# Four graph layers on one core: an attention chunk's accumulators gated while they are copied, drains replaced by semaphores, degrees in three batches

## The reference, cut to what matters

```python
deg = jnp.clip(adj.sum(axis=1), 1.0)
dis = deg ** (-0.5)
adj_norm = dis[:, None] * adj * dis[None, :]
diffusion = adj_norm @ x - x
sim = x @ x.T / (norms[:, None] * norms[None, :])
attn = jax.nn.softmax(beta * sim * adj, axis=1)
return diffusion + jax.nn.sigmoid(alpha) * (attn @ x - x)
```

## Time and profile before

| What | Value |
|---|---|
| median of three runs | 945.01 us (944.57 to 945.73) |
| the profiled execution | 945.11 us, its span 943.3 us |
| mean granted TensorE clock over the span | 0.992 of full speed |
| PE busy | 856.4 us, 91% of the span |
| DVE busy | 642.5 us, 68% |
| ACT busy | 485.7 us, 51% |
| POOL busy | 292.1 us, 31% |
| read from HBM | 69.81 MB |

### The profile page before, as it was taken

One profiled execution on the slowest core, in us unless ns is written; L12 is line 12 of the kernel. 1 busy time (PEld: TensorE's weight loads), 2 busy tenths in 40 slices (PEclk: granted clock), 3 DMA queues, 4 the chain that ended last, 5 costly groups with the idle time before them and its releaser, 6 DMA issues.

```text
span 943.3 us, 18224 instructions
## 1 busy us (share of the span) xinstructions
PE 856.4 (91%) x6496; PEld 509.7 (54%) x6496; DVE 642.5 (68%) x1782; ACT 485.7 (51%) x1020; POOL 292.1 (31%) x380
## 2 busy tenths in 40 slices
PE   0189999999999999979999999999999999999992
PEld 0157676767676767645444445555455555545451
DVE  6989999999999999994344423322135676646576
ACT  5758687878687877653122212111026646525344
POOL 4665454544344544432111210000012222212121
PEclk9999999999999999999999999999999999999996
DMA  8848887988798989200000000000000000000100
GB/s 248 241 125 261 203 247 222 237 226 263 199 251 208 246 224 236 62 1 1 1 1 1 1 1 1 1 1 1 1 1 1 1 1 1 1 1 13 34 23 23
DMA packets 84813, 89.75 MB, mean 95 GB/s; under 512 B 71296, under 2 KB 76544, under 8 KB 76544
## 3 DMA queue, kind: packets, MB, share of 16 engines
q1 hardware_dynamic: 81088, 88.09, 33.7%
q10 hardware_dynamic: 3648, 0.61, 0.4%
HBM read 69.81 MB, written 2.10 MB: 76 GB/s over the span
## 4 chain that ended last, share of the span: by engine, by line
PE 53%; DVE 25%; issue 10%; POOL 4%; DVEq 3%; ACT 2%; DMA 1%; ACTq 0%; POOLq 0%; SPq 0%
PE ps_acc L1234 27%; PE ps_acc L1166 10%; DVE e_parts L762 6%; PE ps_s L1149 6%; DVE ps_s L756 4%; PE ps_t L1234 3%; PE ps_t L1149 3%; POOL att_sb L356 2%; DVE ps_t L756 2%; PE ps_s L1297 1%; DVE ez L689 1%; POOL e_parts L332 1%; PE ps_s L1265 1%; ACT ez L480 1%; DVE x L779 1%
## 5 line engine op out<-in xcount | busy, mean ns | idle before, releaser
L332 POOL CAST e_parts<-ez 128x512 f16<-128x512 f32 x256 | 158.0, 644 | 201.7 <-ACT ez L480 201.7
L1166 PE MATMUL ps_acc<-h_a,e_parts 128*128 128x129 f16 x3072 | 198.6, 220 | 21.6 <-DVE e_parts L762 20.8
L1166 PEld LDWEIGHTS ps_acc<-h_a,e_parts 128*128 128x128 f16 x3072 | 183.7, 97 | 61.4 <-DVE e_parts L762 33.1
L1234 PE MATMUL ps_acc<-adj_t,stage 128*128 128x512 fp8e4 x896 | 198.9, 379 | 0.0
L762 DVE TENSOR_TENSOR e_parts<-ez,e_parts 128x512 f16<-128x512 f32 x256 | 178.3, 735 | 10.3 <-POOL e_parts L332 9.5
L1234 PE MATMUL ps_acc<-adj_t,h_a 128*128 128x512 fp8e4 x768 | 170.3, 379 | 0.0
L434 ACT ACTIVATE bytes<-stage 128x1024 uint8<-128x1024 f32 x128 | 134.1, 1048 | 28.1 <-DMA stage<-in_adj 28.0
L1234 PEld LDWEIGHTS ps_acc<-adj_t,stage 128*128 128x128 f16 x896 | 87.1, 98 | 98.9
L1149 PE MATMUL ps_s<-u_t 128*128 128x512 f16 x516 | 127.0, 383 | 0.0
L480 ACT ACTIVATE ez<-ps_s,scal 128x1024 f32<-128x1024 f32 x86 | 103.1, 1199 | 42.4 <-DVE ps_s L756 40.7
L518 ACT ACTIVATE ez<-x,small 128x128 f32 (+1 forms) x96 | 39.5, 482 | 158.9 <-DVE small L881 158.9
(11 more groups left out here) (164 smaller groups left out, 830.8 us busy)
## 6 DMA issues: line engine op xcount, KB each, us to landing
stage<-in_adj SPq DMA_DIRECT2D x64, 1024.0 KB, 5.7
x<-in_x SPq DMA_DIRECT2D x4, 512.0 KB, 8.3
out<-x SPq DMA_DIRECT2D x8, 256.0 KB, 2.2
adj_t<-bytes SPq DMA_TRANSPOSE x64, 3.1
kernel_sb<-in_L_gnn_kernel ACTq DMA_DIRECT2D x1, 64.0 KB, 7.1
w_sb<-in_L_gnn_W ACTq DMA_DIRECT2D x1, 64.0 KB, 8.1
embed_top<-in_L_gnn_embed ACTq DMA_DIRECT2D x1, 64.0 KB, 8.2
embed_top<-in_L_gnn_layer ACTq DMA_DIRECT2D x1, 64.0 KB, 7.4
```

The costliest lines, as they stand in the source:

```text
L332: g.tensor_copy(e_parts[:, HI, g_s % RING, :], ez[:, g_s % RING, :]).then_inc(ehi_done, 1)
L1166: last = t.matmul(att_acc[:, b, 0:D + 1], e_parts[:, re, g_s % RING, P * b:P * (b + 1)], h_a[:, s, rh, 0:D + 1], start=(s == 0 and n == 0 ...
L1234: last = t.matmul(acc, h[:, k, r, :], adj_f8[:, k // 2, CW * c:CW * (c + 1), k % 2], start=(k == 0 and r == LO), stop=(k == NB - 1 and r = ...
```

## The change

Seven things are done. (1) The evacuation takes the reciprocal of the denominators from the accumulators, and copies the accumulators with the gate `sig_h` applied; both release `acc_free`, so PE's waits count by two. (2) It stands behind the first of the pair's two low parts instead of ahead of both. (3) The tail has only the four updates of `x`; waits on `acc_free`, `x_less` and the new `x_att` take the place of its drains. (4) `x_minus_h` signals `x_less` and has no drain; ACT waits for all eight of them before it casts the quarter that leads to the overwriting of `h0f`. (5) The degrees come in three batches: chunks 0 to 3 at pair 8 of chunk 4, 4 to 6 at pair 8 of chunk 6, chunk 7 at its pair 5. (6) `deg` keeps the unscaled sum; the scaling by 1/64 joins the clipping, and the two later uses. (7) POOL's eight `root_degree` stand at points of chunks 4 to 7 listed in `ROOT_AT`.

```diff
+DEGREES_AT = {(4, 8): (0, 4), (6, 8): (4, 7), (7, 5): (7, 8)}
+ROOT_AT = {(4, 9): 0, (4, 11): 1, (4, 13): 2, (5, 1): 3, (6, 9): 4, (6, 11): 5, (6, 13): 6,
+           (7, 6): 7}
...
             def root_degree(c):
-                pool.wait_ge(pow_in, c + 1)
+                pool.wait_ge(pow_in, 1 if c < 4 else 2 if c < 7 else 3)
                 power(dis[:, BC * c:BC * (c + 1)], neg_half).then_inc(pow_ok, 1)
...
                     high_part(NB * c + s)
-                    if s == (13 if c == NCH - 1 else 19):
-                        root_degree(c)
+                    if s % 2 and (c, s // 2) in ROOT_AT:
+                        root_degree(ROOT_AT[c, s // 2])
...
                 exp_pair(p)
+                if p + CAST_AHEAD == 2 * HPC * (NCH - 1):
+                    act.wait_ge(x_less, NCH)
                 if p + CAST_AHEAD < PAIRS:
                     cast_quarter(p + CAST_AHEAD)
...
             def x_minus_h(c, blocks):
                 v.scalar_tensor_tensor(pairs(x[:, blocks, :]), h0f[:, c, :, :], x_coef,
-                                       pairs(x[:, blocks, :]), ALU.mult, ALU.add)
-                dve.drain()
+                                       pairs(x[:, blocks, :]), ALU.mult, ALU.add
+                                       ).then_inc(x_less, 1)
...
             def att_evac(c):
                 dve.wait_ge(e_used, NB * (c + 1))
-                v.tensor_copy(att_sb[:, :, :], att_acc[:, :, 0:D + 1]).then_inc(acc_free, 1)
-                dve.drain()
+                if c:
+                    dve.wait_ge(x_att, c)
+                v.reciprocal(rec, att_acc[:, :, D]).then_inc(acc_free, 1)
+                v.tensor_scalar(att_sb[:, :, 0:D], att_acc[:, :, 0:D], sig_h, None, ALU.mult
+                                ).then_inc(acc_free, 1)
 
             def att_tail(c):
-                v.reciprocal(rec, att_sb[:, :, D])
-                dve.drain()
-                v.tensor_scalar(rec, rec, sig_h, None, ALU.mult)
-                dve.drain()
+                dve.wait_ge(acc_free, 2 * (c + 1))
+                dve.wait_ge(x_less, min(c + 2, NCH))
                 for b in range(BC):
                     xb = x[:, BC * c + b, :]
-                    v.scalar_tensor_tensor(xb, att_sb[:, b, 0:D], rec[:, b:b + 1], xb,
-                                           ALU.mult, ALU.add)
-                dve.drain()
-
-            def degrees(c):
-                cut = slice(BC * c, BC * (c + 1))
-                dve.wait_ge(cast_done, HPC * (c + 1))
+                    last = v.scalar_tensor_tensor(xb, att_sb[:, b, 0:D], rec[:, b:b + 1], xb,
+                                                  ALU.mult, ALU.add)
+                last.then_inc(x_att, 1)
+
+            def degrees(first, end):
+                cut = slice(BC * first, BC * end)
+                dve.wait_ge(cast_done, HPC * end)
                 v.tensor_reduce(deg[:, cut], deg_parts[:, cut, :], mybir.AxisListType.X,
                                 ALU.add)
                 dve.drain()
-                v.tensor_scalar(deg[:, cut], deg[:, cut], 1.0 / A_BYTE, None, ALU.mult)
-                dve.drain()
-                v.tensor_scalar(dis[:, cut], deg[:, cut], 1.0, None, ALU.max
+                v.tensor_scalar(dis[:, cut], deg[:, cut], 1.0 / A_BYTE, 1.0, ALU.mult, ALU.max
                                 ).then_inc(pow_in, 1)
...
+                low_part(2 * p)
                 if c and k == 0:
                     att_evac(c - 1)
-                low_part(2 * p)
                 low_part(2 * p + 1)
...
-                if k == (5 if c == NCH - 1 else 8):
-                    degrees(c)
+                if (c, k) in DEGREES_AT:
+                    degrees(*DEGREES_AT[c, k])
...
             att_tail(NCH - 1)
+            dve.drain()
...
-            v.tensor_scalar(d2, deg, 1.0, None, ALU.add).then_inc(pow_in, 1)
-            v.tensor_tensor(inv_deg, deg, l1b, ALU.add)
+            v.tensor_scalar(d2, deg, 1.0 / A_BYTE, 1.0, ALU.mult, ALU.add).then_inc(pow_in, 1)
+            v.scalar_tensor_tensor(inv_deg, deg, 1.0 / A_BYTE, l1b, ALU.mult, ALU.add)
...
                 if c and s == 0:
-                    pe.wait_ge(acc_free, c)
+                    pe.wait_ge(acc_free, 2 * c)
```

More of the change, by code:

```diff
@@ L190, in program @@
                  "h_sq_in n_h_ok v_sq_in n_v_ok h2_sq_in n_h2_ok a_sq_in n_a_ok cat_sq_in "
-                 "n_cat_ok tanh_in tanh_out ln_in ln_out h2_ok v_ok v_out split_g diag_hi diag_ok").split()
+                 "n_cat_ok tanh_in tanh_out ln_in ln_out h2_ok v_ok v_out split_g diag_hi diag_ok "
+                 "x_less x_att").split()
         adj_in = [sem("adj_in0"), sem("adj_in1")]
@@ L201, in program @@
          n_cat_ok, tanh_in, tanh_out, ln_in, ln_out, h2_ok, v_ok, v_out, split_g, diag_hi,
-         diag_ok) = (
+         diag_ok, x_less, x_att) = (
             sem(n) for n in names)
@@ L342, in _ @@
                     high_part(NB * c + s)
-                    if s == (13 if c == NCH - 1 else 19):
-                        root_degree(c)
-            pool.wait_ge(pow_in, NCH + 1)
+                    if s % 2 and (c, s // 2) in ROOT_AT:
+                        root_degree(ROOT_AT[c, s // 2])
+            pool.wait_ge(pow_in, 4)
             power(d2, neg_half).then_inc(pow_ok, 1)
@@ L541, in _ @@
             act.wait_ge(s_done, PAIRS)
-            act.wait_ge(pow_in, NCH + 1)
+            act.wait_ge(pow_in, 4)
             for m in (0, 1):
@@ L1209, in aggregate @@
                     elif L == 0 and c < 4:
-                        pe.wait_ge(acc_free, NCH)
+                        pe.wait_ge(acc_free, 2 * NCH)
                     else:
```

## The result

The changed kernel takes 938.5 us in the median of four runs (938.03 to 938.71), the kernel before 945.37 us (944.57 to 946.26): ratio 0.9926, 95% interval 0.9909 to 0.9944. The gain is 6.9 us where 9.5 were forecast; the time lies in the forecast's range. The profiled execution took 938.03 us with a span of 936.3 us. One execution further down, of the kernel with quarter loads and a spread tail, took 948.29 us at a mean granted clock of 0.944 of full speed, where the others show 0.988 to 0.993; no ratio counts it.

What follows compares the result with a forecast made beforehand. PE sets the pace in mid-chunk, DVE's chain at seven chunk starts. Chain 10.4 + x_minus_h 0.9 + degrees 0.5 - loads 2.3 = 9.5 us; 945.1 - 9.5 = 935.6 us, range 931.5 to 941.5.

Steps and rivals of the forecast that it cites:

- The chain at a chunk's start: DVE's work from the evacuation to PE's third pair, seven chunk starts: 7.16 us after the change, gaining 10.4 us in all.
- The length before: Old kernel's time from the evacuation to PE's third pair: mean 8.78 us over seven chunk starts.
- Behind the attention: After the attention stage: one small operation changes, costed at 0.
- The give-back: Adjacency loads, nearly the bound of shorter chunks, take back 0.33 us per chunk, 2.3 us; ends 0 and 7 x 1.
- The third rival: Chunk starts: evacuation waits behind a low part needing POOL's cast and ACT's exponential; 3.5 us slower, 948.6 us; chance 0.05.
- The first rival: Attention chunks: adjacency loads bound them at 44.8 us; gain 6.8 us, 938.3 us; chance 0.13.
- Drains: DVE at evacuation, tail and x_minus_h: each drain costs 0.15 us, which its removal saves.
- the second rival: DVE at chunk starts: drains are free and the tail's 0.4 us POOL wait passes to the updates; 941.2 us; chance 0.11.
- Degrees: DVE's degree batches: hidden in mid-chunk apart from tenths; in chunk 7 an operation and a drain less, 0.5 us gained.
- ACT's new wait: ACT before the cast at (6, 4): under 1 us, once, hidden.

Runs made afterwards that it cites:

- the kernel with quarter loads and a spread tail: Changed kernel with each half loaded as two 512 KB loads, the tail's updates one each in pairs 1 to 4, x_minus_h at pair 9: 925.74 us, ratio 0.9785.
- the kernels with hidden loads: Adjacency loads cut to 512 KB: changed kernel 932.24 us, kernel before 941.73 us; also kernels loading all bytes as two 512 KB loads per half, changed kernel 932.08 us.
- the spread tail: Changed kernel with its own 1 MB loads, the tail's updates spread over pairs 1 to 4 and x_minus_h moved to pair 9: 932.04 us, ratio 0.9841.

## Why the prediction was right, and which terms were not

*The chain at a chunk's start* was right, and the kernels with hidden loads show it by itself. Its sum was 7.16 us and came to 7.30, and the tail is the term that was mis-sized: 1.5 us were taken between ends of 1.15 and 1.9, and 1.77 measured (106.26 to 108.03). The forecast had the cause, a wait for POOL that passes from the scaling to the updates, and took too little of it: 0.27 us short, 1.9 us over seven. Removing the scaling thus saved little of its 0.58 us. The other terms were slightly too dear, 0.13 us in all: evacuation 0.74 against 0.80, the second low part 0.60 against 0.64. The scaled copy, 0.72 us, came close to the plain copy, as taken.

*The length before* was the second mis-sized term. The mean of 8.78 us over seven starts held three starts of 9.00 and 9.16; with loads hidden all are 8.58. The gain of 1.48 us per start was 1.28 (8.58 - 7.30), 1.4 us less over seven, and with x_minus_h 1.45 per chunk (45.13 - 43.68), against 1.6.

*Behind the attention* the forecast put one small operation at nothing. The runs show 0.9 us lost there, with every kernel that has the new evacuation, and not at that operation; this is the third term that was off, and its cause is open. These 0.9 and the 1.4 us of the starts are the whole difference between the forecast's sum before giving back, 11.8 us, and the 9.5 us that the change is worth without loads.

*The give-back* of 2.3 us was right in size, 6.3 - 4.2 = 2.1 by the medians and 5.9 - 3.4 = 2.5 by the spans, but only half in kind. Of its two reasons, a late load that finds no lead at a chunk's start is seen: three of seven starts are longer by 0.56 to 1.17 us, 2.5 us in all, where those of the kernel before were longer by 1.4 in all. The other, loads that nearly bound a chunk, is not: they had cost 3.4 to 4.2 us already with chunks of 45.7 us, and they cost no more with the spread tail's chunks of 43.5 us than in the changed kernel. That the size came out so well is in part luck. The third rival's mechanism, a low part that waits ahead of the evacuation, was seen in a mild form: DVE's idle there fell to none in five of seven starts and PE waited 0.2 to 0.3 us before the first or the second pair in three. That is far below the 1.5 us from which it would have decided.

*The first rival*, chunks at 44.8 us or more, was close: 44.5 in the mean, and its 938.3 us is nearer to the result than the forecast's 935.6. But its reason, loads that set a fixed length, is not what happened: its sign, waits of PE in mid-chunk, reached 0.3 us at most, and with the tail spread the same loads allowed 43.5 us.

*Drains* were as read: no gap is left behind any operation of the evacuation and the tail, so the second rival falls in its first half, and the 7.0 us gained are past the 3.9 that it would have left. (What the forecast calls the next section of the Trainium skill's page "VectorE: DVE Perf Modes" is its section "Two Vector instructions with no wait between them".) Its second half came true: the updates took over the scaling's wait for POOL, 1.84 us instead of 1.39. What is done besides the order (drains, gated copy, shorter tail, x_minus_h, degrees) is worth 5 us, the order 4; the drains were not run apart from the rest, so their share is read from the gaps in the timelines alone. *Degrees*: hidden in mid-chunk, as costed at nothing; in chunk 7 the step fell from 1.20 us to 0.64, 0.5 forecast. *ACT's new wait* took 0.7 us, once. DVE in chunk 7:

```profile
385.57 0.15 DVE L795 TENSOR_REDUCE cols<-deg_parts 128x4 f32<-128x16 f32 x1
...
386.21 1.22 DVE L762 TENSOR_TENSOR ps_t<-ps_t,adj_t 128x1024 f32<-128x1024 f32 x1
```

## What to carry to other kernels

Where two engines run at nearly the same pace, look at the points where one has extra work: there each of its microseconds counts, and elsewhere hardly any did here. A better remedy than making the extra work cheaper was to spread it, in pieces that fit into what the engine regains per step: with one update in it DVE's pair takes 2.60 us (from the update at 190.98 to the next at 193.58) instead of 2.34, and PE's takes 2.67. A mean over starts that a third resource disturbs hides what the chain itself costs: hide that resource once (shorter loads), measure, and only then add up parts.

## What was not expected of the hardware

Two loads of 512 KB with a semaphore each, landing in 4.8 us in the median, the first of them issued a pair earlier, hid what one load of 1 MB, landing in 5.7 us, could not, with the same bytes and the DMA share up from 0.87 to 0.92. The engines had room; the buffer's turn was too long. Issuing the 1 MB load ahead of the transpose, which holds SP for 1.24 us, moved the wait and gained nothing: loads landed in 5.4 us, but transposes in 6.2 instead of 3.1 (DMA share 0.96).

An update of 128 x 128 on DVE, with two inputs in SBUF, takes 0.34 us, and 0.69 when it starts early in a cast of POOL; where the cast had 0.23 us left, it took 0.37.
